# Reordering the set-up of a four-layer conditioned sequence kernel: two load queues, weight scaling on ScalarE, and a wait moved into the main program

## What is computed

```
x = L0(x, cond, mask0)   # 16 heads, linear attention: softmax of q over a head's columns, of k over the rows
x = L1(x, cond, mask1)   # 16 heads, full softmax attention
x = L2(x, cond)          # two state-space scans (forward and backward), 512 channels, 16 states
x = L3(x, cond, mask2)   # 8 heads, linear attention

# the parts of L0 (L1 and L3 alike) that the set-up prepares
xn = layernorm(x) * norm_scale + norm_bias
q, k, v = xn @ Wq + bq, xn @ Wk + bk, xn @ Wv + bv      # rows masked in k and v
scale, shift = split(silu(cond) @ film_W + film_b)      # per sequence
y = layernorm(attention(q, k, v)) * film_scale + film_bias
x = x + silu(y * (1 + scale) + shift) @ Wo + bo
```

## Time and profile before

| what | value |
|---|---|
| median of 3 runs | 4430.05 us (4429.83 to 4433.16) |
| profiled execution | 4430.37 us, span 4428.6 us |
| busy: PE, DVE, ACT, POOL | 3722.4, 4050.2, 3609.1, 3849.4 us |
| DMA | 462.12 MB, mean 104 GB/s |
| first instruction of the main program | 80.44 us |

### The profile page before, as it was taken

The page is one execution under the profiler, slowest core; times in us unless marked ns, Lnnn a source line. Parts: engine busy times, 40 slices in busy tenths (PEclk is TensorE's granted clock), DMA queues, the critical chain, the costliest instruction groups (busy, mean ns, idle before and its releaser), DMA issues.

```text
span 4428.6 us, 74058 instructions
## 1 busy us (share of the span) xinstructions
PE 3722.4 (84%) x26464; PEld 2478.3 (56%) x26464; DVE 4050.2 (91%) x5619; ACT 3609.1 (81%) x8678; POOL 3849.4 (87%) x1772
## 2 busy tenths in 40 slices
PE   5988888889888888888888888888888888888664
PEld 3665555556565555555555555555655555556432
DVE  4449999989999999999999999999999999999995
ACT  0368878878988899889888998898888988988763
POOL 0019988989999999999999999999999999999994
PEclk6899999989999999999999999999999999999876
DMA  4033444543444445434444444344444444444541
GB/s 122 11 75 91 94 105 95 118 113 82 117 117 114 109 113 120 111 91 112 117 117 112 110 117 117 91 106 117 117 114 107 117 117 103 94 117 114 123 107 32
DMA packets 334160, 462.12 MB, mean 104 GB/s; under 512 B 56204, under 2 KB 165847, under 8 KB 333789
## 3 DMA queue, kind: packets, MB, share of 16 engines
q1 hardware_dynamic: 333632, 457.32, 43.7%
q10 hardware_dynamic: 158, 0.08, 0.0%
HBM read 370.26 MB, written 86.50 MB: 103 GB/s over the span
## 4 chain that ended last, share of the span: by engine, by line
ACT 28%; DVE 18%; PE 18%; POOL 7%; issue 5%; DMA 2%; SPq 0%; POOLq 0%; ACTq 0%; DVEq 0%
ACT ps L706 11%; PE ps L171 10%; DVE ps L721 5%; POOL S_X L767 5%; ACT A_ring L472 3%; DVE A_sm L429 3%; DVE S_X L721 3%; PE ps L804 3%; DVE S_X L736 2%; POOL S_X L780 2%; PE ps L376 2%; ACT C_xh L154 1%; PE ps L545 1%; ACT T_v L303 1%; DVE C_dd L579 1%
## 5 line engine op out<-in xcount | busy, mean ns | idle before, releaser
L767 POOL TENSOR_TENSOR S_X<-S_slot,S_bc 128x1024 f32<-128x1024 f32 x1024 | 2403.2, 2366 | 174.8 <-PE ps L804 119.2
L706 ACT ACTIVATE ps<-S_slot,acol 128x256 f32<-128x256 f32 x4096 | 1742.7, 468 | 190.5 <-DVE S_X L736 180.8
L721 DVE TENSOR_TENSOR_SCAN ps<-ps,S_X 128x512 f32<-128x512 f32 x1088 | 1300.0, 1214 | 37.4 <-POOL S_X L767 19.6
L780 POOL TENSOR_TENSOR S_X<-S_X,S_bc 128x1024 f32<-128x1024 f32 x480 | 1132.6, 2366 | 38.7 <-DVE S_X L721 32.6
L721 DVE TENSOR_TENSOR_SCAN S_X<-ps,S_X 128x512 f32<-128x512 f32 x960 | 1141.2, 1208 | 16.3 <-ACT ps L706 13.7
L736 DVE TENSOR_TENSOR S_X<-ps,S_bc 128x512 f32<-128x512 f32 x1088 | 712.5, 675 | 5.7 <-issue 0.2
L804 PE MATMUL ps<-S_X,sum 128*32 128x256 f32 x8192 | 615.6, 403 | 102.6 <-POOL S_X L780 62.4
L804 PEld LDWEIGHTS ps<-S_X,sum 128*32 128x32 f32 x8192 | 198.9, 112 | 388.8 <-issue 169.2
L429 DVE TENSOR_REDUCE A_sm<-ps 128x4 f32<-128x1024 f32 x256 | 311.0, 1215 | 62.7 <-PE ps L376 59.5
L376 PE MATMUL ps<-A_kP,A_qP 32*128 32x256 f32 x2048 | 292.7, 403 | 45.5 <-DVE A_sm L429 31.4
L395 PE MATMUL ps<-A_qP,A_kP 32*128 32x256 f32 x2048 | 296.7, 407 | 21.6 <-ACT A_ring L472 15.2
(11 more groups left out here) (295 smaller groups left out, 6882.0 us busy)
## 6 DMA issues: line engine op xcount, KB each, us to landing
S_slot<-scr_dd SPq DMA_DIRECT2D x1024, 256.0 KB, 4.7
scr_dd<-C_dd SPq DMA_DIRECT2D x64, 1024.0 KB, 5.3
S_bc<-scr_bc SPq DMA_DIRECT2D x256, 256.0 KB, 6.3
L_xin<-in_x SPq DMA_DIRECT2D x32, 256.0 KB
scr_x<-A_x SPq DMA_DIRECT2D x32, 256.0 KB, 5.8
T_x<-scr_x SPq DMA_DIRECT2D x32, 256.0 KB
out_x<-xs SPq DMA_DIRECT2D x32, 256.0 KB, 6.1
T_gate<-scr_gate SPq DMA_DIRECT2D x32, 128.0 KB
```

Source lines behind the costliest of these rows:

```text
L706: ins = a.activation(B["bank"][half_at(b, u, i)][:, n * T:(n + 1) * T], B["slot"][:, s, j, 0, :], ACT.Exp, scale=K.k["acol"][:, s, LINES * ...
L721: v.tensor_tensor_scan(line(x if u in ON_POOL else decay), line(decay), line(x), 0.0, ALU.mult, ALU.add).then_inc(S.scan.sem, 1)
L767: g.tensor_tensor(B["X"][:, u % RING], B["slot"][:, s, :, 1, :], rep(B["bc"][:, s, q, :], 1, LINES), ALU.mult).then_inc(S.b.sem, 1)
L780: g.tensor_tensor(B["X"][:, u % RING], B["X"][:, u % RING], rep(B["bc"][:, s, NQ + q, :], 1, LINES), ALU.mult).then_inc(S.cp.sem, 1)
```

## The change

- SP no longer waits for VectorE's memsets before its loads. The three masks, the condition and the film vectors and weights are now issued by ScalarE on its queue (16 loads), the rest by SP (57 loads, and the first sequence). The conditions stage is cut in three: masks, conditions, ada.
- ScalarE scales the projection weights (18 instructions); VectorE doesn't any more.
- VectorE does the memsets of `bias`, of the mask rows and of `dbc`, the mask arithmetic and the split of the masks ahead of its wait for the attention loads. The bias split moves from before layer L0's film columns to before layer L1's.
- The bias chain moves from ScalarE's queue to SP's, where it stands behind all of SP's loads.
- The store of `pcol` is no longer waited for at the end of the set-up but by SP in the main program, before it loads the first `pcol` rows. VectorE waits for `xin` alone, TensorE for the other two loads ahead of the k projection.
- The main program's memsets shrink to two on `vA`; the wait of all engines for them is gone (ScalarE alone waits for them, before it first writes `vA`).

```diff
 def pe_linear(p, K, B, L, dh, b):
...
     p.wait_ge(S.dve.sem, S.dve.at(b, "qsub"))
+    if L == "L0":
+        p.wait_ge(K.land["a"].sem, K.land["a"].at(b))
     for c in range(KD):
...
 def act_softmax(a, K, b):
...
     a.wait_ge(S.pe.sem, S.pe.at(b, "v"))
+    if b == 0:
+        a.wait_ge(K.ready, 2)
...
 def l_dve(v, K, b):
     yield
-    v.wait_ge(K.land["a"].sem, K.land["a"].at(b))
+    v.wait_ge(K.land["xin"].sem, K.land["xin"].at(b))
...
 def l_sp(q, K, b):
...
-    q.dma_start(B["xin"][:], K.x_in[b].rearrange("(t p) d -> p t d", p=P)).then_inc(K.land["a"].sem, 16)
+        q.dma_start(B["xin"][:], K.x_in[b].rearrange("(t p) d -> p t d", p=P)).then_inc(K.land["xin"].sem, 16)
+    else:
+        q.wait_ge(K.W.columns, 16)
     q.dma_start(B["pc"][:, 0:8], K.scr["pcol"][b][:, 0:8]).then_inc(K.land["a"].sem, 16)
     q.dma_start(B["omL0"][PARTS:2 * PARTS, :], K.scr["mask"][b][0]).then_inc(K.land["a"].sem, 16)
...
-LOADS = {"attention": 31, "conditions": 21, "scans": 21}
+LOADS = {"attention": 31, "masks": 3, "conditions": 13, "ada": 5, "scans": 21}
...
         @block.vector
...
+            mark["padded"] = t.n
+            where = k["bias"][0:2 * PARTS, sections["L1k"]]
+            t.count(t.ready().memset(k["bias"][:], 0.0))
+            t.count(t.ready().memset(k["bias"][0:2 * PARTS, :], 1.0))
...
+            for om in K.omL:
+                t.count(t.ready().memset(om[:], 0.0))
+                t.count(t.ready().memset(om[0:PARTS, :], 1.0))
+            t.count(t.ready().memset(K.dbc[ONE:ONE + 1, :], 1.0))
+            pc, mf, mr = M["pcol"], M["mf"], M["mr"]
+            t.ready().wait_ge(got["masks"], 16 * LOADS["masks"])
...
+            split(lambda i: M["mparts"][:, :, i, :], mr[:], M["mback"][:])
+            mark["mparts"] = t.n
             t.ready().wait_ge(got["attention"], 16 * LOADS["attention"])
             for L in ATTENTION:
                 for m in "qkv":
...
-                    for i in range(KD):
-                        dst, src = k[L + "w" + m][:, i, :], M[L + m + "raw"][:, i, :]
-                        t.count(t.ready().tensor_scalar(padded_heads(dst) if padded else dst, heads(src) if padded else src, M[L + "g"][:, i:i + 1], None, ALU.mult))
...
             v.wait_ge(got["conditions"], 16 * LOADS["conditions"])
-            v.wait_ge(scalar, 3)
+            v.wait_ge(scalar, 3 * KD * len(ATTENTION) + 3)
...
             for L, (_, _, _, _, at) in FILM.items():
-                if L == "L3":
-                    split(lambda i: M["mparts"][:, :, i, :], mr[:], M["mback"][:])
-                    mark["mparts"] = t.n
+                if L == "L1":
+                    v.wait_ge(round1, 16)
+                    split(lambda i: M["bparts"][:, i, :], M["rowsb"][:], M["back"][:])
+                    mark["bparts"] = t.n
...
         @block.scalar
         def _(a):
...
+                load(a, "masks", M["mi"][:], W["mask_BxS_ik0"])
...
+                load(a, "conditions", M["cond"][:], W["cond_2048"])
...
+                for L in FILM:
+                    load(a, "conditions", M[L + "fw"][:], tiles("%s_cond_%s" % (L, FILM[L][0])))
             a.preload_act_table_set(ACT_SET)
+            a.wait_ge(vector, mark["padded"])
+            a.wait_ge(got["attention"], 16 * LOADS["attention"])
+            for L in ATTENTION:
+                for m in "qkv":
...
+                    for i in range(KD):
...
+                        t.count(a.activation(padded_heads(dst) if padded else dst, heads(src) if padded else src, ACT.Copy, scale=M[L + "g"][:, i:i + 1]))
+            a.wait_ge(vector, mark["mparts"])
             a.wait_ge(got["conditions"], 16 * LOADS["conditions"])
...
-            t.ready().wait_ge(vector, mark["allb"])
-            a.dma_start(scr["bias"].rearrange("(a n) -> a n", a=1), M["allb"][:]).then_inc(round3, 16)
...
         @block.sync
...
-                q.wait_ge(vector, 12)
...
+                q.dma_start(K.xin[:], K.x_in[0].rearrange("(t p) d -> p t d", p=P)).then_inc(K.land["xin"].sem, 16)
...
             assert asked == LOADS, asked
+            q.wait_ge(vector, mark["allb"])
+            q.dma_start(scr["bias"].rearrange("(a n) -> a n", a=1), M["allb"][:]).then_inc(round3, 16)
+            q.wait_ge(round3, 16)
+            q.dma_start(M["rowsb"][:], scr["bias"].rearrange("(a n) -> a n", n=P)).then_inc(round1, 16)
             q.wait_ge(vector, mark["mparts"])
             q.dma_start(scr["mask"], M["mparts"][:]).then_inc(stored, 16)
+            q.wait_ge(vector, mark["bparts"])
+            q.dma_start(scr["bparts"].rearrange("i (a n) -> a i n", n=P), M["bparts"][:]).then_inc(round2, 16)
+            q.wait_ge(round2, 16)
+            q.dma_start(k["bias"][0:PARTS, :], scr["bparts"]).then_inc(stored, 16)
             q.wait_ge(vector, mark["pcol"])
-            q.dma_start(scr["pcol"].rearrange("b p n -> p b n"), M["pcol"][:]).then_inc(stored, 16)
-            q.wait_ge(stored, 16 * 3)
+            q.dma_start(scr["pcol"].rearrange("b p n -> p b n"), M["pcol"]).then_inc(K.W.columns, 16)
+            q.wait_ge(stored, 16 * 2)
...
 def bass_kernel(nc, W, out):
...
                 v.memset(K.A["vA"][:], 0.0).then_inc(K.ready, 1)
-                for om in (K.L["omL0"], K.A["omL1"], K.T["omL3"]):
-                    v.memset(om[:], 0.0).then_inc(K.ready, 1)
-                v.memset(K.C["dbc"][ONE:ONE + 1, :], 1.0).then_inc(K.ready, 1)
-                v.wait_ge(K.ready, 5)
+                v.wait_ge(K.ready, 1)
                 v.memset(K.A["vA"][:, :, :, DH1:DH1 + 1], 1.0).then_inc(K.ready, 1)
...
             def _(p):
-                p.wait_ge(K.ready, 9)
                 program(p, K, "PE")
```

More of the change, by code:

```diff
@@ L1069, in setup_weights, with load @@
         made, vector, scalar, masks = sem("set_pe"), sem("set_dve"), sem("set_act"), sem("set_pool")
-        got = dict(K.W.got, attention=sem("set_ld_attention"), conditions=sem("set_ld_conditions"))
+        got = dict(K.W.got, **{n: sem("set_ld_" + n) for n in ("attention", "masks", "conditions", "ada")})
         round1, round2, round3, stored = sem("set_round1"), sem("set_round2"), sem("set_round3"), sem("set_stored")
-        mark = {}
+        mark, asked = {}, {}
+        def load(e, stage, dst, src):
+            e.dma_start(dst, src).then_inc(got[stage], 16)
+            asked[stage] = asked.get(stage, 0) + 1
         block = ctx.enter_context(nc.Block())
@@ L1174, in _ @@
             mark["pcol"] = t.n
-            t.ready()
+            t.ready().wait_ge(got["ada"], 16 * LOADS["ada"])
         @block.tensor
@@ L1226, in _ @@
-            a.wait_ge(round2, 16)
-            a.dma_start(k["bias"][0:PARTS, :], scr["bparts"]).then_inc(stored, 16)
+            t.ready()
         @block.sync
         def _(q):
-            asked = {}
-            def load(stage, dst, src):
-                q.dma_start(dst, src).then_inc(got[stage], 16)
-                asked[stage] = asked.get(stage, 0) + 1
             with nc.allow_non_contiguous_dma(reason="columns of bias vectors, once"):
-                q.wait_ge(vector, 12)
                 for L, ns in ATTENTION.items():
@@ L1240, in _ @@
                     a = ["%s_cond_%s" % (L, n) for n in ns]
-                    load("attention", M[L + "g"][:], cols(a[0]))
-                    load("attention", M[L + "b"][:], cols(a[1]))
+                    load(q, "attention", M[L + "g"][:], cols(a[0]))
+                    load(q, "attention", M[L + "b"][:], cols(a[1]))
                     for n, m in ((2, "q"), (4, "k"), (6, "v")):
-                        load("attention", M[L + m + "raw"][:], tiles(a[n]))
-                        load("attention", M["L1%sb" % m][:] if L == "L1" and m != "v" else M["allb"][0:1, sections[L + m]], line(a[n + 1]))
@@ L1246, in _ @@
-                    load("attention", k[L + "wo"][:], tiles(a[8]))
-                    load("attention", M["allb"][0:1, sections[L + "o"]], line(a[9]))
-                load("attention", M["allb"][0:1, sections["wf"]], line("L2_cond_bf"))
-                load("conditions", M["cond"][:], W["cond_2048"])
-                for L, (w, b, s, t, _) in FILM.items():
-                    load("conditions", M[L + "fb"][:], cols("%s_cond_%s" % (L, b)))
-                    load("conditions", M[L + "fs"][:], cols("%s_cond_%s" % (L, s)))
-                    load("conditions", M[L + "ft"][:], cols("%s_cond_%s" % (L, t)))
-                    load("conditions", M[L + "fw"][:], tiles("%s_cond_%s" % (L, w)))
@@ L1255, in _ @@
-                load("conditions", M["mi"][:], W["mask_BxS_ik0"])
-                load("conditions", M["mf"][:, 1, :], W["mask_BxS_ff1"])
-                load("conditions", M["mf"][:, 2, :], W["mask_BxSx1_fk1"].rearrange("b t a -> b (t a)"))
-                load("conditions", M["wada"][:], W["L2_cond_Wada"].rearrange("(m p) k -> p m k", p=P))
-                load("conditions", M["bada"][:], line("L2_cond_bada"))
-                load("conditions", M["badac"][:], cols("L2_cond_bada"))
```

(11 more changed lines are left out.)

79 lines of the change are left out of this document (39 added, 40 removed).

## The result

| | before | after |
|---|---|---|
| median, same chip | 4431.6 us (4429.83 to 4439.83, 4 runs) | 4401.3 us (4392.54 to 4406.88, 4 runs) |
| profiled execution | 4430.37 us, span 4428.6 us | 4404.70 us, span 4403.0 us |
| first instruction of the main program | 80.44 us | 59.80 us |
| VectorE's first copy there | 84.47 us | 61.07 us |
| first statistics of the first sequence | 88.05 us | 64.47 us |

The ratio is 0.9926, 95% interval 0.9904 to 0.9948. The sign was right. The profiled executions differ by 25.7 us, of which 23.6 (88.05 less 64.47) have been gained by the first statistics, where 14.9 were forecast.

A forecast was written before the change was run, and what follows sets the result against it. Loads fill the set-up from 10 to 58 us, and SP's wait for pcol's store ends it. An earlier start (12.5 us) plus VectorE's earlier copies (2.4) make 14.9 us off 4430.4, forecast 4415, range 4405 to 4422.

The forecast's parts named there:

- The added waits: Main program: SP's wait for pcol's store before its loads costs nothing, with 14 us of cover before the k projection.
- The bias chain, moved to SP: End of set-up: chain leaves at 47.2, lands at 67.4, main program starts at 67.9, 12.5 us earlier.
- a sign of being wrong: Main program's start: the forecast is wrong if it comes after 72 or before 64 us.
- they aren't the gate: Set-up: film products run from 35 to 56 us but don't decide when the set-up ends.
- The second queue itself is then worth about 1 us: Set-up loads: of the 7.1 us by which SP is free earlier, about 1 us comes from the second queue.
- Scaling on ScalarE, masks and memsets are costed at nothing: Set-up: this work, up to 9 us on ScalarE and 20 on VectorE, is covered until 47.2 us.
- The load of `xin` gives nothing by itself: Start of main program: loading the first sequence earlier gains nothing, as it was hidden behind VectorE's copies.
- rival (c): After the start: the gain is absorbed later in a strand paced by another, 4430 us, chance 0.04.
- Rival (b): Set-up: the loads don't end sooner, chain and start come 7.1 us later, 4422 us, chance 0.10.
- what the forecast allowed for this distance: From main program's start to kernel's end: 4348.2 us before, to change by no more than 2.4 us.
- (a): Early main program: more gained as TensorE's clock may rise to 2.4 GHz, 8 us, giving 4407, chance 0.17.
- (d): Main program, 140 to 180 us: TensorE's clock may stay at 1.2 GHz, slower, 4455 us, chance 0.05.

The follow-up runs named there:

- chain_on_act: Changed kernel with the bias chain back on ScalarE's queue, behind the sigmoid; median 4396.06 us, ratio 0.993 to the kernel before.
- one_queue: Changed kernel with ScalarE's 16 loads moved to SP's queue behind the attention loads, bias chain on SP; median 4409.48 us, ratio 0.9941 to before.
- one_queue_chain_act: Changed kernel with all loads on SP's queue and the bias chain on ScalarE's; median 4400.61 us, ratio 0.9947 to before.
- three_parts: Kernel before with early SP loads, pcol's store awaited in the main program, and its mask-row and dbc memsets moved into set-up; 4411.18 us, ratio 0.996.
- only_columns: Kernel before with only the wait for pcol's store moved into the main program; median 4419.08 us, ratio 0.9979.
- again: The changed kernel once more, unaltered; median 4400.73 us, ratio 0.9934 to the kernel before.
- only_early: Kernel before with only SP's wait for the memsets ahead of its loads removed, still one queue; median 4419.96 us, ratio 0.9979.
- split_late: Changed kernel with the mask split moved back to just ahead of layer L3's film columns; median 4408.98 us, ratio 0.9952 to before.
- wide_film: Changed kernel with film weights moving 512 columns against a stationary condition, products then turned back; median 4399.68 us, ratio 0.9924 to before.

## Why the prediction was right and wrong

**Right.** The start is earlier because of the early loads (8.0 us measured alone) and because nobody waits for `pcol`'s store (8.1 alone). VectorE's copies come 1.3 us behind the start, 1.6 were forecast: 2.8 us gained for 2.4. The film products were forecast from 35 to 56 and ran from 37.1 to 56.4 (behind attention loads that landed at 24.9, not 22). The added waits cost nothing: the k projection came at 82.62, 10 us or more behind SP's loads for it (the wait of 8.6 us ends about 68, and with 4.2 us for the loads, the bound that the forecast took, they land by about 72.6).

**Wrong: "The bias chain, moved to SP".** This step put the start at 67.9, and it came at 59.80, below the 64 that the forecast named as a sign of being wrong. Each duration of the chain was read from the earlier trace rows, where loads still ran beside it. In the new order the chain runs while the last loads end and behind them. The table gives the steps in us and in brackets the share of the DMA engines over each (before from 43.3 to 49.0, 49.0 to 53.0 and 54.9 to 59.5 us, the changed kernel from 44.2 to 48.1, 48.1 to 49.8 and 51.7 to 53.1). That the load makes the difference and not the queue is seen in `chain_on_act`: on ScalarE's queue, as before, its steps are long while loads run (4.6 and 5.5 at 1.06) and the last one short behind them (1.4 at 0.08).

| step of the chain | taken | changed kernel | under load elsewhere |
|---|---|---|---|
| SP free | 47.2 | 44.2 | 51.0 (`one_queue`) |
| store to reload | 5.7 (0.95) | 3.85 (0.72) | 4.6 (1.06, `chain_on_act`) |
| reload to VectorE | 4.0 (0.86) | 1.8 (0.37) | 5.5 (1.06, `chain_on_act`) |
| second store to its successor | 4.6 (0.67) | 1.4 (0.08) | 3.1 (0.75, `one_queue_chain_act`) |

Of the chain's steps these are 3.0 + 1.85 + 2.2 + 3.2 = 10.3 us too many (the 44.2 through the loads' higher rate, a share of 1.04 where 0.95 was taken and 1 was taken as the bound). With them gone the chain would end at 57.1 even with the 4.0 us taken for its last landing, which no row shows. It ends first, and the gate is the one that the forecast had as second, 3 us behind: `pcol`. It was forecast complete at 64.4, because the bias split was put at 56.9 and layer L1's and L3's columns behind it. The split came at 49.84, so VectorE was done with it and with L1's columns at 54.03, while TensorE was at L3's products until 56.4. L3's last columns and the masks followed, and `pcol` was complete at 58.94. So both candidates for the end hung on the same misread durations. What holds in their place is the film products' end, which the forecast had nearly right (56 for 56.4) and of which it said "they aren't the gate".

**"The second queue itself is then worth about 1 us": undersized.** Without it SP's last load goes out 7.2 us later. It is worth 5.3 us of the start in this order (`one_queue`), and 0 with the chain elsewhere.

**"Scaling on ScalarE, masks and memsets are costed at nothing": wrong for two.** With film products as the gate the early split is worth 4.7 us and the scaling 3.9. Their stated cover, SP's issuing until 47.2, wasn't what ended the set-up.

**"The load of `xin` gives nothing by itself": wrong in combination.** Alone it would give nothing. With the start earlier it is uncovered: 3.65 us in `three_parts`, 1.44 in `only_columns`.

Not all single effects are a sum: 8.1 + 8.0 bring the start to 64.87 with the memsets, and the last 5.1 us to 59.80 need the split, the scaling and, since the chain went to SP, the second queue together. Each of them undone alone brings back 3.9 to 5.3 us.

**Sums of the forecast.** Its bounds add up to about 4409 to 4419, where it says 4411 to 4419, and the barrier is 0.40 us by its own numbers, not 0.45. Neither changes the outcome.

**The rest of the 30 us.** The trace shows 23.6 us at the first statistics. By the store that ends layer L1 for sequence 8 (at 1238.43 before, 1215.28 after) the lead is 23.2, so nothing is absorbed and rival (c) falls. Rival (b), whose 7.1 us are the end of SP's issues before (54.3) less the forecast 47.2, falls with the last load at 43.31. From the start of the main program to the end of the span it is 4343.2 us, 5.0 less than before, of which 2.8 are VectorE's. That is 2.6 us beyond what the forecast allowed for this distance. From the medians it is 30 us; the interval of the ratio allows 23 to 43, and the second measurement (`again`) gives 27.6. The scatter has a visible companion, TensorE's granted clock. The mean granted clock in the 220 us from the first statistics, and the distance from these to that store:

| profile | clock | distance us |
|---|---|---|
| after | 0.83 | 1150.8 |
| `only_early` | 0.83 | 1150.7 |
| before | 0.86 | 1150.4 |
| `again` | 0.89 | 1137.9 |
| `chain_on_act` | 0.91 | 1142.0 |
| `only_columns` | 0.92 | 1142.9 |
| `split_late` | 0.93 | 1135.5 |

Over all 14 profiles the time at the low level there (31 to 75 us) and the distance go together (correlation 0.84, 0.31 us for each us), but loosely: `one_queue_chain_act` has 0.89 as `again` has, and 1145.0 us. `again` is the changed kernel too, so the same program gets 0.83 in one run and 0.89 in another. So rivals (a) and (d) describe something that exists, but what is shown is a scatter of the runs, not an effect of the change: in the changed kernel's first profile TensorE still ran at 0.50 from 70 to 80 us, while in `again` the k projection came at 79.20 with 1.00 granted (79 to 82 us), and the runs of before scatter as widely. That the clock causes it was not tried, as no kernel here sets the clock alone, and what decides the level in a run stays open. Whether the 6 us between 23.6 and 30 are this or chance stays open as well.

## What to carry to other kernels

A transfer's duration belongs to the load on the DMA engines in the row where it is read: the second store of the chain took 4.6 us at a share of 0.67 and 1.4 us at 0.08. When a chain of small dependent transfers is moved behind the loads, take its steps from an idle stretch, or give both ends. Before one strand is called the gate, work out the end of each other one without it, since here three strands (chain, film products, VectorE's serial tail) ended within a few us and each edit only handed the end to the next. And where single runs scatter by 10 us, read a set-up change at a fixed mark of the timeline: start and first statistics repeated within 0.8 us.

## What the hardware showed that was not expected

- TensorE was busy for 19.88 of 20 us with products of 32 columns and its granted clock was 0.54 there (the changed kernel from 37 to 57 us; 0.50 from 46 to 60). The same products as 512 moving columns ran at 1.00, busy 10.82 of 11 us (`wide_film`). So two stretches equally busy in the records got different levels. They differ in the weight loads beside the products (PEld 19.82 of 20 us against 2.96 of 11). Whether the width of the products or their weight loads matter was not tried.
- The profile gives the clock as a share only, and every sum here uses the ratio of the two levels alone. What the names 1.2 and 2.4 GHz have behind them in the trace is a rate: in the kernel before, a bf16 product of 256 columns gave way to the next one after 0.21 us at 0.50 (96.15 to 96.36) and after 0.11 us at 1.00 (146.64 to 146.75), about 1.2 and 2.3 columns a ns.
- Two queues gave 357 GB/s and a share of 1.08 from 10 to 20 us, one queue 152 GB/s and 0.64. The loads as a whole are the same, but not those of the stretch: on one queue the 1 MB loads stood behind small ones.
- The store of the bias parts (30x3x128 bf16, 23 KB) with its completion took 3.1 to 5.4 us while loads ran or had just been issued (3.1 in `one_queue_chain_act` at a share of 0.75, 4.6 before at 0.67, 5.4 in `three_parts` at 0.61) and 1.4 us at 0.08 when they were done, on either queue. Among the three long ones the share doesn't give the order.
- Three runs of before within 3.3 us (4429.83 to 4433.16) hid a scatter of 25 us that 23 runs showed (4420.28 to 4444.89).
